# Layer 2's gather, its side bias and its scores at other places in a software-pipelined graph network kernel

## The chip, the cores and the metric

The kernel runs on one core of one Trainium2 chip. The metric is the device time of one execution in microseconds. The core has five instruction queues that run side by side and wait for each other through semaphores: TensorE (PE; its weight loads are listed apart, as PEld), VectorE (DVE), ScalarE (ACT), GpSimd (POOL) and SyncE (SP), which here only issues DMAs.

## The reference

128 graphs of 128 nodes with 384 features go through two layers of the same kind, then a residual and a layer norm.

```python
def layer(h, params):                       # h: (128, 128, 384), scanned over 2 layers
    u = einsum('bid,bjd->bij', h, h) / sqrt(D)
    a = softmax(u, axis=-1)
    delta = a * adjacency_matrix
    attn = delta / (sum(delta, axis=-1, keepdims=True) + 1e-10)
    hl, hs, hr = h @ wl.T + b_l, h @ ws.T + b_s, h @ wr.T + b_r
    ctx = (attn * upper) @ hl + diagonal(attn)[..., None] * hs + (attn * lower) @ hr
    o = (ctx - mean) / sqrt(var + 1e-12) * g + beta
    return relu(o)
out = layernorm(x + layer2(layer1(x)))      # eps 1e-5
```

All is float32. The products are formed from a high and a low part of each operand (three matmuls for one).

## The kernel before

**Tiling.** One graph is one unit of work. Per graph and layer TensorE runs 27 projection matmuls of 128 by 384: nine for each of UP, LOW and SELF (three chunks of the features, three high/low terms). UP and LOW are called the sides; they use two banks of `p_proj`, SELF a third. There are three score matmuls (128 by 256) and six gather matmuls (128 by 384), which multiply the two masked, transposed halves of the attention with the projected sides.

**Software pipeline.** Every engine has its own `iteration(i, r)`, written out by hand for the first and last iterations and rolled (four at a time) between. Iteration i works on several graphs at once: layer 1's projections of graph i, its early scores of i + 2 and i + 3, layer 2's projections of graph i - 3, its scores of i - 2, its gather of i - 4 and its output of i - 4 and i - 5. The order within a queue is the order in which the code issues; a wait holds all that is behind it in the same queue. Iterations 0 to 3 (`fill`) and from 127 on (`close`) have orders of their own. The steady order holds for iterations 4 to 126.

**TensorE's order** in one iteration: 18 side projections of layer 1 with two scores of graph i + 2 between them (`score_early`); 9 self projections of layer 1 with the three scores of layer 2 of graph i - 2 after the first, second and third (`score_late`, which first waits for `s_lo[1]`, the low part of hT of layer 2); 9 side projections of layer 2; layer 2's gather of i - 4; the other 9 side projections, with the first score of graph i + 3 after the first of them; 9 self projections of layer 2; layer 1's gather of i. A gather waits for the low attention half (`s_side_lo`, GpSimd L1300), the low projections (`s_proj_lo`, GpSimd L299), and the use of its former result.

**VectorE's order:** rows of layer 1 of graph i - 1 (L698 writes `gathered`, L702, L704, L711, L717), `low_rows` (L754), the bias of layer 1's sides (L767, which also moves them from PSUM to SBUF), the two scaled scores (L778), block transposes and masks (L817, L802, L807, L790), diagonals (L812), the bias of layer 1's self projection (L771), then `row_moments`, `row_variance` and `centre_layer2` of layer 2 (L698, L702, L704, L711, L725), the bias of layer 2's sides (L767), `output_rows` (L733, L739; it waits for the root that GpSimd computes, L1304, from what L711 wrote), and the bias of layer 2's self projection (L771).

**ScalarE's order:** `relu_rows` (L1083, three), `high_rows` (L1094), `normalise_rows` (L1066), exponentials, high halves of the attention, copies, `high_projections` of layer 1 (L1062), `keep_high` (L1033, L1034), DMA issues, the next input, squared denominators (L1099), `output_squares` (L1121, L1126), `finish` (L1066), and `high_projections` of layer 2 (L1062).

**GpSimd's order:** low projections of layer 2 (L299), root and bias for layer 1's norm (L1304, L1308), L1356, L1294 twice, low attention halves (L1300) of layer 2 and layer 1, low projections of layer 1 (L299), the root of layer 2 (L1304), the root and bias of the output (L1304, L1308), low input (L1330).

So `low_rows` hangs on this: layer 2's rows and output stand ahead of layer 1's rows in VectorE's queue, those ahead of `low_rows`, and the first layer 2 score of TensorE waits for that.

Of the kernel before, what the change touches and what calls it, by code (L numbers as in the profile page):

```python
# [52 lines left out]
def graph_block(nc: bass.Bass, xT: bass.AP, x: bass.AP, adj: bass.AP, WT: bass.AP, bias: bass.AP,  # L53
# [9 lines left out]
    with ExitStack() as ctx:  # L63
# [390 lines left out]
        def _(pe):  # L454
# [44 lines left out]
            def score_late(b1, slot1, n):  # L499

                if n == 0:
                    done(pe, s_lo[1], b1)
                    if not isinstance(b1, int) or b1 > 2:
                        done(pe, s_kept, b1 - 3)
                if n < C:
                    step = score_step(1, b1, slot1, n)
                    if n == C - 1:
                        step.then_inc(s_parts[1], 1)

            def project_sides(k, b, slot, before, b_last, steps, scored=None, first=0, last_part=14,  # L510
                              early=None):

                if 0 in steps:
                    done(pe, s_biased[before], b_last)
                for n in steps:
                    if isinstance(b, int) and b == 0 and n % 3 == 0:

                        pe.wait_ge(s_w_lo[k][UP + n // 9], n % 9 // 3 + 1)
                    last = project_step(k, b, slot, UP + n // 9, n % 9)
                    if early is not None and (n, early[2]) == (9, 0):
                        score_early(early[0], early[1], 0)
                    if early is not None and n in (1, 3, 5) and early[2] > 0 and n // 2 + early[2] <= C:
                        score_early(early[0], early[1], n // 2 + early[2] - 1)
                    if scored is not None:
                        score_slice(*scored, n, first, last_part)
                if 17 in steps:
                    last.then_inc(s_proj[k], 1)  # L530

            def project_self(k, b, slot, before, b_last, scored=None, first=0, last_part=8, late=None):
                done(pe, s_self_biased[before], b_last)
                for n in range(9):
                    if isinstance(b, int) and b == 0 and n % 3 == 0:
                        pe.wait_ge(s_w_lo[k][SELF], n // 3 + 1)
                    last = project_step(k, b, slot, SELF, n)
                    if late is not None:
                        score_late(*late, n)
                    if scored is not None and n < 8:  # L540
                        score_slice(*scored, n, first, last_part)
                last.then_inc(s_self[k], 1)
                if scored is not None:
                    score_slice(*scored, 8, first, last_part)
# [122 lines left out]
            def iteration(i, r):  # L667
                p, q = r % 2, 1 - r % 2
                if filling(i):
                    fill(i, p)  # L670
                elif closing(i):
                    close(i, p)
                else:
                    alone = isinstance(i, int) and i < 6
                    rest = (i + 2, (r + 2) % 4, 1 if alone else 2) if live(i, i + 2) else None
                    first = (i + 3, (r + 3) % 4, 0) if live(i, i + 3) and not (isinstance(i, int) and i < 5) else None
                    project_sides(0, i, r, 1, i - 4, range(18), early=rest)
                    project_self(0, i, r, 1, i - 4, late=(i - 2, p))
                    project_sides(1, i - 3, q, 0, i, range(9))
                    gather(1, i - 4)  # L680
                    project_sides(1, i - 3, q, 0, i, range(9, 18), early=first)
                    project_self(1, i - 3, q, 0, i)
                    gather(0, i, True)

            run(pe, iteration)
# [2 lines left out]
        def _(dve):  # L688
# [68 lines left out]
            def add_bias(k, b, sides_too):  # L757
# [4 lines left out]
                if sides_too:  # L762
                    if k == 0 and isinstance(b, int) and 0 < b < 4:

                        done(dve, s_proj_lo[0], b - 1)
                    done(dve, s_proj[k], b)
                    nc.vector.tensor_tensor(proj[u][:, UP:LOW + 1, :], p_proj[:, UP:LOW + 1, 0:D],  # L767
                                            bias_all[:, k, UP:LOW + 1, :], ALU.add).then_inc(s_biased[k], 1)
# [206 lines left out]
            def iteration(i, r):  # L975
# [24 lines left out]
                if live(i, i + 1):  # L1000
                    diagonal(0, i + 1, q)
                add_bias(0, i, False)
                row_moments(1, i - 4, p)
                row_variance(1, i - 4, p).then_inc(s_veps[1], 1)
                centre_layer2(i, i - 4)
                add_bias(1, i - 3, True)
                output_rows(i - 4, p)
                add_bias(1, i - 3, False)

# [3 lines left out]
        def _(act):  # L1013
# [41 lines left out]
            def high_projections(k, b):  # L1055
# [3 lines left out]
                if k == 0 and isinstance(b, int) and 0 < b < 4:  # L1059

                    done(act, s_gather[0], b - 1)
                nc.scalar.activation(proj_split[u][:, HI], proj[u][:, UP:LOW + 1, :],  # L1062
                                     ACT.Copy).then_inc(s_proj_hi[k], 1)

# [192 lines left out]
            def iteration(i, r):  # L1257
# [23 lines left out]
                if live(i, i + 1):  # L1281
                    squared_denominators(0, i + 1, q)
                squared_denominators(1, i - 3, q)
                if live(i, i - 5):
                    output_squares(i - 5, q)
                    finish(i, q)
                high_projections(1, i - 3)

            run(act, iteration)

# [187 lines left out]
```

## Time and profile before

| | |
|---|---|
| three runs | 1613.95 us median (1612.61 to 1614.08) |
| the profiled execution | 1614.73 us, span 1613.0 us |
| TensorE | 1594.6 us busy (99%), 9267 matmuls |
| VectorE | 1396.4 us (87%) |
| GpSimd | 1294.1 us (80%) |
| ScalarE | 1079.3 us (67%) |
| granted TensorE clock | 0.997 of full speed |
| DMA | 131 GB/s over the span |

The span runs from the first to the last instruction; the execution's own time has a little around it. Busy time counts each engine by itself. Matmuls are pipelined: one of 128 by 384 is recorded as about 0.34 us long and the next starts some 0.17 us after it, so their spacing is to be read from starts, and a stall can lie inside what is shown as busy. On VectorE too an operation may start before the one ahead of it has ended. In the timeline, equal instructions in a row are merged, and brackets give the idle time before a group and what released it.

### The profile page before, as it was taken

The page shows a single profiled execution, that of the slowest core. Times are in us where ns is not written, and L with a number is a line of the kernel's source. Part 1 is how long each engine was busy: PE and PEld are TensorE (multiplying, and loading weights), DVE is VectorE, ACT ScalarE, POOL GpSimd, SP SyncE. Part 2 cuts the span into 40 slices and gives each one's busy share as a digit, 9 for nine tenths or more (in the row PEclk, how much of TensorE's full clock was granted, in tenths as well). Part 3 has the DMA queues.
Part 4 walks back from the last instruction along what each step waited for, and adds up shares of the span by engine and source line. Part 5 has one row for each costly group of instructions (what it writes and reads, how often), then busy time and mean ns, then how long its engine had stood idle before and what let it go on. Part 6 is the DMA issues. An engine that isn't in the chain of part 4 may idle for free.

```text
span 1613.0 us, 35972 instructions
## 1 busy us (share of the span) xinstructions
PE 1594.6 (99%) x9267; PEld 1571.5 (97%) x9267; DVE 1396.4 (87%) x4490; ACT 1079.3 (67%) x2958; POOL 1294.1 (80%) x1665
## 2 busy tenths in 40 slices
PE   9999999999999999999999999999999999999996
PEld 8999999999999999999999999999999999999995
DVE  7788888888888888888888888888888888888887
ACT  6566666666666666666666666666666666666665
POOL 6788888888888888888888888888888888888874
PEclk9999999999999999999999999999999999999998
DMA  5555555555555555555555555555555555555541
GB/s 180 125 132 138 129 133 135 132 133 130 134 132 135 129 137 131 133 130 139 127 133 130 138 129 133 133 134 133 130 134 131 135 129 139 130 133 129 135 108 49
DMA packets 589175, 211.28 MB, mean 131 GB/s; under 512 B 473952, under 2 KB 572256, under 8 KB 589152
## 3 DMA queue, kind: packets, MB, share of 16 engines
q1 hardware_dynamic: 490752, 198.91, 47.8%
q10 hardware_dynamic: 98400, 12.11, 4.9%
q8 instruction: 9, 0.15, 0.0%
q14 instruction: 14, 0.11, 0.0%
HBM read 128.98 MB, written 81.92 MB: 131 GB/s over the span
## 4 chain that ended last, share of the span: by engine, by line
PE 97%; DVE 1%; POOL 1%; ACT 1%; issue 0%; DMA 0%; SPq 0%; DVEq 0%; POOLq 0%; ACTq 0%
PE p_proj L464 74%; PE p_gather L591 17%; PE p_score L458 5%; DMA w_raw<-WT 0%; POOL proj_split L299 0%; POOL w L1351 0%; DVE proj L767 0%; DVE p_gather L725 0%; DVE p_gather L733 0%; DVE stats L702 0%; DVE p_gather L698 0%; ACT proj_split L1062 0%; PE p_score L482 0%; DVE y L739 0%; POOL rstd L1304 0%
## 5 line engine op out<-in xcount | busy, mean ns | idle before, releaser
L464 PE MATMUL p_proj<-w,hT_layer 128*128 128x384 f32 x6912 | 1345.7, 338 | 0.0
L464 PEld LDWEIGHTS p_proj<-w,hT_layer 128*128 128x128 f32 x6912 | 1193.7, 188 | 0.5 <-POOL w L1351 0.3
L299 POOL TENSOR_TENSOR proj_split<-proj,proj_split 128x768 fp32r<-128x768 f32 x253 | 467.1, 1846 | 88.4 <-ACT proj_split L1062 88.4
L591 PE MATMUL p_gather<-proj_split,attnT_split 128*128 128x384 f32 x1536 | 322.5, 344 | 2.2 <-issue 2.2
L767 DVE TENSOR_TENSOR proj<-p_proj,bias_all 128x768 f32<-128x768 f32 x256 | 243.9, 953 | 71.6 <-PE p_proj L464 71.6
L1300 POOL TENSOR_TENSOR attnT_split<-attnT,attnT_split 128x256 fp32r<-128x256 f32 x256 | 190.2, 743 | 142.8 <-ACT attnT_split L1053 142.7
L591 PEld LDWEIGHTS p_gather<-proj_split,attnT_split 128*128 128x128 f32 x1536 | 263.0, 188 | 21.8 <-POOL attnT_split L1300 14.3
L1304 POOL TENSOR_TENSOR rstd<-veps,neg_half 128x1 f32<-128x1 f32 x384 | 208.7, 549 | 52.7 <-DVE veps L711 39.6
L1062 ACT ACTIVATE proj_split<-proj 128x768 fp32r<-128x768 f32 x256 | 213.0, 832 | 5.8 <-DVE proj L767 4.8
L458 PE MATMUL p_score<-hT_layer 128*128 128x256 f32 x768 | 215.6, 281 | 1.1 <-DVE hT_layer L754 0.8
L1066 ACT ACTIVATE normed<-gathered,nbias,rstd 128x384 f32<-128x384 f32 x128 | 90.7, 709 | 141.5 <-POOL nbias L1308 141.5
L1294 POOL TENSOR_TENSOR attnT<-whole,sides 128x256 f32<-128x256 f32 x249 | 179.1, 741 | 0.6 <-DMA whole<-swap_mem 0.6
L1066 ACT ACTIVATE o<-y,nbias,rstd 128x384 f32<-128x384 f32 x128 | 90.8, 709 | 132.5 <-POOL nbias L1308 132.5
L1133 ACT ACTIVATE hT_layer<-xt_raw 128x384 fp32r<-128x384 f32 x128 | 67.1, 525 | 141.5 <-issue 140.3
L1083 ACT ACTIVATE p_rows<-rowsT,shift,gain 128x128 f32<-128x128 f32 x369 | 149.5, 444 | 0.0
L458 PEld LDWEIGHTS p_score<-hT_layer 128*128 128x128 f32 x768 | 144.2, 188 | 1.9 <-DVE hT_layer L754 1.1
L1039 ACT ACTIVATE p_score<-scores,rows 128x128 f32<-128x128 f32 x256 | 92.7, 362 | 76.6 <-DVE rows L778 76.5
L771 DVE TENSOR_TENSOR proj<-p_proj,bias_all 128x384 f32<-128x384 f32 x256 | 141.5, 553 | 2.0 <-PE p_proj L464 1.9
L1330 POOL TENSOR_TENSOR hT_layer<-xt_raw,hT_layer 128x384 fp32r<-128x384 f32 x128 | 131.5, 1028 | 4.9 <-ACT hT_layer L1133 4.9
L802 DVE CUSTOM_DVE_ANT_0 attn<-p_score,adj_layer 128x128 f32<-128x128 f32 x256 | 70.8, 277 | 45.1 <-ACT p_score L1039 42.9
L1053 ACT ACTIVATE attnT_split<-attnT 128x256 fp32r<-128x256 f32 x256 | 103.2, 403 | 0.5 <-DVE attnT L831 0.5
L698 DVE SCALAR_TENSOR_TENSOR p_gather<-proj,rows,p_gather 128x384 f32<-128x384 f32 x128 | 79.6, 622 | 19.2 <-PE p_gather L591 12.1
(69 smaller groups left out, 1677.7 us busy)
## 6 DMA issues: line engine op xcount, KB each, us to landing
swap_mem<-blocks SPq DMA_DIRECT2D x124, 256.0 KB, 2.2
whole<-swap_mem SPq DMA_DIRECT2D x496, 64.0 KB, 2.5
xt_raw<-xT SPq DMA_DIRECT2D x128, 192.0 KB, 2.6
xn<-x SPq DMA_DIRECT2D x128, 192.0 KB, 2.6
out<-o SPq DMA_DIRECT2D x128, 192.0 KB, 2.0
rows_mem<-rows_blocks SPq DMA_DIRECT2D x123, 192.0 KB, 1.9
adj_layer<-adj SPq DMA_DIRECT2D x256, 64.0 KB, 2.1
rowsT<-rows_mem SPq DMA_DIRECT2D x246, 48.0 KB, 2.5
```

The source lines that it names most:

```text
L299: op.tensor_tensor(proj_split[u][:, LO], proj[u][:, UP:LOW + 1, :], proj_split[u][:, HI].bitcast(F32), ALU.subtract).then_inc(s_proj_lo[k], 1)
L458: return nc.tensor.matmul(parts[k], h[:, slot, HI, n, :], h[:, slot, HI:LO + 1, n, :], start=(n == 0), stop=(n == C - 1))
L464: return nc.tensor.matmul(p_proj[:, which, 0:D], hT_of(k, b)[:, slot, st, c, :], w[:, k, which, mv, c, :], start=(n == 0), stop=(n == 8))
L591: last = nc.tensor.matmul(home(k, b)[:, 0:D], AT_split[u][:, st, side, :], proj_split[u][:, mv, side, :], start=(side == UP and n == 0), s ...
L767: nc.vector.tensor_tensor(proj[u][:, UP:LOW + 1, :], p_proj[:, UP:LOW + 1, 0:D], bias_all[:, k, UP:LOW + 1, :], ALU.add).then_inc(s_biased ...
L771: nc.vector.tensor_tensor(proj[u][:, SELF, :], p_proj[:, SELF, 0:D], bias_all[:, k, SELF, :], ALU.add).then_inc(s_self_biased[k], 1)
L1062: nc.scalar.activation(proj_split[u][:, HI], proj[u][:, UP:LOW + 1, :], ACT.Copy).then_inc(s_proj_hi[k], 1)
L1066: nc.scalar.activation(rows_out, rows_in, ACT.Identity, bias=nbias[:, which:which + 1], scale=rstd[:, which:which + 1]).then_inc(s_rows, 1)
L1083: last = nc.scalar.activation(relu_T[:, c, :], rows_in[:, c, :], ACT.Relu, bias=shift1[:, c:c + 1], scale=gain1[:, c:c + 1])
L1294: nc.gpsimd.tensor_tensor(AT[k][:], whole[:, k].unsqueeze(1).broadcast_to([P, 2, N]), sides[:], ALU.mult).then_inc(s_side[k], 1)
L1300: nc.gpsimd.tensor_tensor(AT_split[u][:, LO], AT[u][:], AT_split[u][:, HI].bitcast(F32), ALU.subtract).then_inc(s_side_lo[k], 1)
L1304: return nc.gpsimd.tensor_tensor(rstd[:, which:which + 1], veps[:, which:which + 1], neg_half[:], ALU.pow)
```

## The change

Four edits. On TensorE layer 2's gather goes behind all 18 side projections of layer 2; the first score of graph i + 3 goes from the tenth side projection to behind the second self projection of layer 2; the three scores of layer 2 go from behind self projections 0, 1 and 2 of layer 1 to behind side projection 16 and self projections 0 and 2. On VectorE the bias of layer 2's sides goes ahead of `row_moments` of layer 2, with a wait for GpSimd's low projections of the graph before, which read the tile that it writes. On ScalarE `high_projections` of layer 2 goes ahead of `output_squares` and `finish`, with a wait for the gather of the graph before, which reads the tile that it writes.

```diff
                     done(pe, s_lo[1], b1)
                     if not isinstance(b1, int) or b1 > 2:
                         done(pe, s_kept, b1 - 3)
-                if n < C:
-                    step = score_step(1, b1, slot1, n)
-                    if n == C - 1:
-                        step.then_inc(s_parts[1], 1)
+                step = score_step(1, b1, slot1, n)
+                if n == C - 1:
+                    step.then_inc(s_parts[1], 1)
             def project_sides(k, b, slot, before, b_last, steps, scored=None, first=0, last_part=14,
-                              early=None):
+                              early=None, late=None):
@@ -520,23 +519,25 @@
                         pe.wait_ge(s_w_lo[k][UP + n // 9], n % 9 // 3 + 1)
                     last = project_step(k, b, slot, UP + n // 9, n % 9)
-                    if early is not None and (n, early[2]) == (9, 0):
-                        score_early(early[0], early[1], 0)
-                    if early is not None and n in (1, 3, 5) and early[2] > 0 and n // 2 + early[2] <= C:
+                    if early is not None and n in (1, 3, 5) and n // 2 + early[2] <= C:
                         score_early(early[0], early[1], n // 2 + early[2] - 1)
+                    if late is not None and n == 16:
+                        score_late(*late, 0)
                     if scored is not None:
                         score_slice(*scored, n, first, last_part)
                 if 17 in steps:
                     last.then_inc(s_proj[k], 1)
-            def project_self(k, b, slot, before, b_last, scored=None, first=0, last_part=8, late=None):
+            def project_self(k, b, slot, before, b_last, scored=None, first=0, last_part=8, early=None, late=None):
                 done(pe, s_self_biased[before], b_last)
                 for n in range(9):
                     if isinstance(b, int) and b == 0 and n % 3 == 0:
                         pe.wait_ge(s_w_lo[k][SELF], n // 3 + 1)
                     last = project_step(k, b, slot, SELF, n)
-                    if late is not None:
-                        score_late(*late, n)
+                    if early is not None and n == 1:
+                        score_early(*early, 0)
+                    if late is not None and n in (0, 2):
+                        score_late(*late, 1 + n // 2)
                     if scored is not None and n < 8:
                         score_slice(*scored, n, first, last_part)
                 last.then_inc(s_self[k], 1)
@@ -673,13 +674,12 @@
                 else:
                     alone = isinstance(i, int) and i < 6
                     rest = (i + 2, (r + 2) % 4, 1 if alone else 2) if live(i, i + 2) else None
-                    first = (i + 3, (r + 3) % 4, 0) if live(i, i + 3) and not (isinstance(i, int) and i < 5) else None
-                    project_sides(0, i, r, 1, i - 4, range(18), early=rest)
+                    first = (i + 3, (r + 3) % 4) if live(i, i + 3) and not (isinstance(i, int) and i < 5) else None
+                    project_sides(0, i, r, 1, i - 4, range(18), early=rest, late=(i - 2, p))
                     project_self(0, i, r, 1, i - 4, late=(i - 2, p))
-                    project_sides(1, i - 3, q, 0, i, range(9))
+                    project_sides(1, i - 3, q, 0, i, range(18))
                     gather(1, i - 4)
-                    project_sides(1, i - 3, q, 0, i, range(9, 18), early=first)
-                    project_self(1, i - 3, q, 0, i)
+                    project_self(1, i - 3, q, 0, i, early=first)
                     gather(0, i, True)
             run(pe, iteration)
@@ -763,6 +763,8 @@
                     if k == 0 and isinstance(b, int) and 0 < b < 4:
                         done(dve, s_proj_lo[0], b - 1)
+                    if k == 1:
+                        done(dve, s_proj_lo[1], b - 1)
                     done(dve, s_proj[k], b)
                     nc.vector.tensor_tensor(proj[u][:, UP:LOW + 1, :], p_proj[:, UP:LOW + 1, 0:D],
                                             bias_all[:, k, UP:LOW + 1, :], ALU.add).then_inc(s_biased[k], 1)
@@ -1000,10 +1002,10 @@
                 if live(i, i + 1):
                     diagonal(0, i + 1, q)
                 add_bias(0, i, False)
+                add_bias(1, i - 3, True)
                 row_moments(1, i - 4, p)
                 row_variance(1, i - 4, p).then_inc(s_veps[1], 1)
                 centre_layer2(i, i - 4)
-                add_bias(1, i - 3, True)
                 output_rows(i - 4, p)
                 add_bias(1, i - 3, False)
@@ -1059,6 +1061,8 @@
                 if k == 0 and isinstance(b, int) and 0 < b < 4:
                     done(act, s_gather[0], b - 1)
+                if k == 1:
+                    done(act, s_gather[1], b - 1)
                 nc.scalar.activation(proj_split[u][:, HI], proj[u][:, UP:LOW + 1, :],
                                      ACT.Copy).then_inc(s_proj_hi[k], 1)
@@ -1281,10 +1285,10 @@
                 if live(i, i + 1):
                     squared_denominators(0, i + 1, q)
                 squared_denominators(1, i - 3, q)
+                high_projections(1, i - 3)
                 if live(i, i - 5):
                     output_squares(i - 5, q)
                     finish(i, q)
-                high_projections(1, i - 3)
             run(act, iteration)
```

## Rows read from the trace of the kernel before

**Rows 1.** Windows, the middle 400 us: each engine's busy us (count), granted clock, DMA.
```profile
400.00:800.00 400.00, 400.00 (x2333) 395.10 (x2333) 351.21 (x1130) 271.45 (x746) 328.54 (x422) 1.00 0.54 132
```
**Rows 2.** The page's costliest groups: the gathers' weight loads; busy, mean, idle before.
```profile
L591 PEld LDWEIGHTS p_gather<-proj_split,attnT_split 128*128 128x128 f32 x1536 | 263.0, 188 | 21.8 <-POOL attnT_split L1300 14.3
```
**Rows 3.** TensorE's timeline (start, length), iterations 6 and 125.
```profile
72.99 0.28 PE L458 MATMUL p_score<-hT_layer 128*128 128x256 f32 x1
...
1543.77 0.28 PE L458 MATMUL p_score<-hT_layer 128*128 128x256 f32 x1
```
**Rows 4.** TensorE's timeline, one iteration from 1012.34.
```profile
1012.34 0.28 PE L458 MATMUL p_score<-hT_layer 128*128 128x256 f32 x1
...
1013.04 2.81 PE L464 MATMUL p_proj<-w,hT_layer 128*128 128x384 f32 x15
1015.69 1.30 PE L591 MATMUL p_gather<-proj_split,attnT_split 128*128 128x384 f32 x6
1016.83 0.34 PE L464 MATMUL p_proj<-w,hT_layer 128*128 128x384 f32 x1
...
1017.13 3.12 PE L464 MATMUL p_proj<-w,hT_layer 128*128 128x384 f32 x17
1020.08 1.20 PE L591 MATMUL p_gather<-proj_split,attnT_split 128*128 128x384 f32 x6
```
**Rows 5.** Timeline of TensorE's weight loads, the same iteration and the next score.
```profile
1015.68 0.99 PEld L591 LDWEIGHTS p_gather<-proj_split,attnT_split 128*128 128x128 f32 x6 [0.15 <-POOL attnT_split L1300]
...
1024.50 0.19 PEld L458 LDWEIGHTS p_score<-hT_layer 128*128 128x128 f32 x1
```
**Rows 6.** GpSimd's timeline, the same iteration.
```profile
1014.89 0.74 POOL L1300 TENSOR_TENSOR attnT_split<-attnT,attnT_split 128x256 fp32r<-128x256 f32 x1 [0.51 <-ACT attnT_split L1053]
...
1019.07 1.07 POOL L1304 TENSOR_TENSOR rstd<-veps,neg_half 128x1 f32<-128x1 f32 x2 [0.32 <-DVE veps L711]
1020.22 0.19 POOL L1308 TENSOR_TENSOR nbias<-neg_mean,rstd 128x1 f32<-128x1 f32 x1
...
1022.02 1.85 POOL L299 TENSOR_TENSOR proj_split<-proj,proj_split 128x768 fp32r<-128x768 f32 x1 [0.65 <-ACT proj_split L1062]
```
**Rows 7.** VectorE's timeline, the same iteration.
```profile
1012.36 0.96 DVE L767 TENSOR_TENSOR proj<-p_proj,bias_all 128x768 f32<-128x768 f32 x1 [0.55 <-PE p_proj L464]
...
1017.13 0.62 DVE L698 SCALAR_TENSOR_TENSOR p_gather<-proj,rows,p_gather 128x384 f32<-128x384 f32 x1 [0.22 <-PE p_gather L591]
...
1018.78 0.21 DVE L711 TENSOR_SCALAR veps<-eps_units,moments 128x1 f32<-128x1 f32 x1
...
1019.43 0.95 DVE L767 TENSOR_TENSOR proj<-p_proj,bias_all 128x768 f32<-128x768 f32 x1
1020.30 0.62 DVE L733 SCALAR_TENSOR_TENSOR p_gather<-p_gather,rstd,shift 128x384 f32<-128x384 f32 x1
...
1023.62 0.56 DVE L754 TENSOR_TENSOR hT_layer<-p_rows,hT_layer 128x384 fp32r<-128x384 f32 x1
```
**Rows 8.** The tail, window 1580 to 1590, columns as in rows 1.
```profile
1580.00:1590.00 10.00, 8.13 (x48) 7.32 (x47) 7.56 (x25) 5.85 (x17) 6.25 (x7) 1.00 0.21 66
```
**Rows 9.** TensorE's timeline in that window.
```profile
1588.46 0.39 PE L458 MATMUL p_score<-hT_layer 128*128 128x256 f32 x1 [0.76 <-DVE hT_layer L754]
```
**Rows 10.** ScalarE's timeline, the iteration of rows 4.
```profile
1018.44 0.60 ACT L1121 ACTIVATE spread<-y,neg_mean 128x384 f32<-128x384 f32 x1
...
1019.16 0.29 ACT L1126 ACTIVATE veps<-y_squares,out_eps 128x1 f32<-128x1 f32 x1
1020.50 0.71 ACT L1066 ACTIVATE o<-y,nbias,rstd 128x384 f32<-128x384 f32 x1 [1.05 <-POOL nbias L1308]
1021.12 0.83 ACT L1062 ACTIVATE proj_split<-proj 128x768 fp32r<-128x768 f32 x1
1021.85 1.22 ACT L1083 ACTIVATE p_rows<-rowsT,shift,gain 128x128 f32<-128x128 f32 x3
1023.10 0.49 ACT L1094 ACTIVATE hT_layer<-p_rows 128x384 fp32r<-128x384 f32 x1
```

## The prediction

> **What bounds the kernel now.** I read the windows first. In the middle 400 us TensorE is busy all the time at a granted clock of 1.00 (its level of 2.4 GHz), VectorE 351 us, GpSimd 329 us, ScalarE 271 us [rows 1]. So the order of TensorE's stream is the kernel, and any time in which it runs without a gap can only be shortened by a gap that "busy" hides. The costliest groups show one: the weight loads of the gathers were idle 21.8 us, 14.3 of it for GpSimd's attnT_split [rows 2]. TensorE's timeline gives the loop: the first layer 2 score of iteration 6 starts at 72.99, that of iteration 125 at 1543.77, so 1470.78 / 119 = 12.36 us each [rows 3]. Inside one iteration [rows 4] projections follow each other at 2.65 / 15 = 0.177 or 2.95 / 17 = 0.174 us, a score 0.12 (1017.13 - 1016.83, less one projection). Layer 2's gather (x6 at 1015.69) is 1.30 us long, layer 1's (x6 at 1020.08) 1.20, by the same six matmuls. The 0.10 is the late weight load: it starts at 1015.68 after 0.15 idle, released by the GpSimd operation that ends at 1014.89 + 0.74 = 1015.63 [rows 5, 6]. That is the only repeated stall of TensorE: 0.10 x 123 = 12 us, 0.8% of the time.
>
> VectorE is next, and its order matters more than its share. One loop of it [rows 7] idles 0.55 ahead of the bias of layer 1's sides (L767, for TensorE), and then runs nearly without a gap to low_rows (L754), which ends at 1023.62 + 0.56 = 1024.18. The weight load of the first layer 2 score, which needs it, starts at 1024.50 [rows 5]. So the slack of that hand-over is 0.32 us.
>
> **The change, part by part.**
> *Gather of layer 2 behind all 18 side projections.* Its GpSimd input has been ready since 1015.63, and the gather would begin nine projections later: the stall goes, -0.10 an iteration. The number of matmuls is unchanged (54 + 12 + 6). For VectorE the gather's result comes later, and that is not hidden by itself; it is in the sum below.
>
> *VectorE: bias of layer 2's sides ahead of layer 2's rows.* In order on VectorE now: bias of layer 1's own projection (L771), bias of layer 2's sides, and then row_moments (L698), variance, centre, output rows, L771, row_moments of layer 1, low_rows. The bias waits for TensorE's 18th side projection and L698 for the gather behind that. All that stands behind L698 in VectorE's queue waits with it: the output, the bias that frees p_proj, layer 1's rows, and low_rows. The added wait on s_proj_lo[1] is for a GpSimd operation of the iteration before, ended some 4 us earlier in the loop (1022.02 + 1.85 there); I cost it at nothing, with one wait step of 0.10 as its other end.
>
> *First layer 2 score two projections earlier* (behind n = 16 of the sides, the others behind n = 0 and 2 of the self projection). The last of the three stays where it was, so the ScalarE copies behind it don't move; but the first now wants low_rows 2 x 0.175 = 0.35 us sooner. The slack of 0.32 is gone by this edit alone. The bias of layer 1's sides comes one score, 0.12, later.
>
> *Chunk 0 of layer 1's early score* moves from the tenth side projection to n = 1 of the self projection. It waits for keep_high, whose ScalarE copies are at the start of the loop's middle; it comes later, and gets only more cover. Nothing.
>
> *ScalarE: high_projections of layer 2 ahead of output_squares and finish, with a wait for the gather of layer 2.* The queue behind it is output_squares, finish, relu_rows, high_rows; priced under the rivals. SP's queue isn't reordered: its out transfer waits for finish and goes out later, and xn behind it is wanted an iteration later.
>
> **The sum: one loop from the first layer 2 score to the next.** All times are counted from that score's start, with durations of the kernel before.
> 1. To the start of the gather's last matmul: 3 scores x 0.12, and 28 projections (the last of the sides, 9 self, 18 of layer 2's sides) and 5 gather matmuls x 0.175: 0.36 + 5.78 = 6.14 [rows 4].
> 2. From there to L698: before, the last gather matmul started at 1016.83 - 0.18 = 1016.65 and L698 at 1017.13: 0.48. Sum 6.62 [rows 4, 7]. VectorE is free by then: the sides' bias starts at 6.14 - 6 x 0.175 + 0.37 = 5.46 and takes 0.87 (1019.43 to 1020.30), so 6.33.
> 3. From L698 to the output rows (L733): without a wait 1019.43 - 1017.13 = 2.30. But L733 needs GpSimd's root. Before, the bias of the sides stood between and hid it. Now: L698 to variance (L711) 1018.78 - 1017.13 = 1.65, to the root's start 0.29, the root 0.55 (two take 1.07), and the release 0.14 (as from the gather's end, 1015.69 + 1.30 = 1016.99, to L698): 2.63. Sum 9.25 [rows 6, 7].
> 4. L733 to the end of low_rows: 1023.62 - 1020.30 + 0.56 = 3.88. Sum 13.13 [rows 7].
> 5. Release of the weight load 0.05 (1015.63 to 1015.68), and 0.11 from a held load to its matmul: a score that waited for this same L754 near the end took 0.39 where others take 0.28. Sum 13.29 [rows 5, 9].
>
> TensorE alone would be back at that score after 12.26 us, so it would stand still there for 1.03 us in each iteration, and the sum is 13.29 - 12.36 = +0.93 an iteration. The check from the other side, counted from an iteration's first projection: the gather and with it L698 come 9 x 0.175 - 0.10 = 1.47 later, the bias that no longer stands between gives back 0.87, the root costs 0.33, so low_rows is 0.93 late; the score is 0.35 early, the loop without its stall 0.10 shorter, and 0.32 of slack is used up: a stall of 1.06, and +0.96 an iteration with the stall that is gone. The two agree to 0.03.
>
> Iterations 4 to 126 have this order, so there are 122 loops: 122 x 0.93 = 113. The profiled execution took 1614.7 (span 1613.0), 0.8 above the median of the runs; 1614.7 + 113 - 0.8 = 1727 us.
>
> Ends: if the root is not waited for (2.30 in step 3) and all matmuls keep to 0.173, the loop is 12.90, +0.54 x 122 = +66: 1680. If two of the new waits cost a step of 0.10 more each, 13.50: +139, 1753. I take the middle reckoning because each of its steps has a row of its own kind.
>
> **A rule weighed.** In the tail of this trace TensorE was busy 8.13 us of a stretch of 10, with a wait of 0.76 before one score, and the granted clock stayed 1.00 [rows 8, 9]. The Trainium skill, "TensorE: Matmul & The Clock Gate", section "A second HAM failure mode: psum-queue depth-cycling", says that small idle gaps between groups of matmuls, if frequent, can make the clock swing between its two levels. By the row the 1.03 us gap costs itself alone; by the rule more, and that is the last rival.
>
> **The rivals.**
> *ScalarE's chain sets low_rows instead.* Behind the gather (6.14 + 0.34 + 0.07 = 6.55): high_projections 0.73, squares 0.72 + 0.29, ready at 8.29; GpSimd's two roots start at 6.62 + 1.65 + 0.29 = 8.56, nbias 1.15 later and 0.19 long, 9.90; finish starts at 9.99, relu_rows 0.62 later, high_rows 1.25 after that and 0.49 long: 12.35 [rows 6, 10]. Low_rows could start at 12.38, where VectorE itself comes at 12.57. If the root's wait in step 3 is smaller than reckoned, VectorE comes at 12.24 and this chain sets the loop: 13.10, +0.74 x 122 = +90, 1704. For: it is only 0.19 behind. Same sign.
> *Faster.* Place: the first layer 2 score. If low_rows is in time for it, TensorE never stops and the gain is the old stall, 0.10 x 122 = 12 us: 1602. The point from which it decides: the slack is 0.32 - 0.35 - 0.10 = -0.13, so low_rows would have to end 0.13 us earlier in the iteration than now, and every 0.01 us later than that costs 1.2 us in all. For it speaks the idle 0.55 ahead of L767, which says that VectorE has time to give; against, that this idle lies behind low_rows, and the waits added are ahead of it.
> *Next to no change.* With VectorE's new order free of cost, the score held by its own shift alone (0.13), the loop would be 12.26 + 0.13 = 12.39: +0.03 x 122 = 4, 1618.
> *The clock swings.* Were a tenth of an iteration's 66 wide matmuls at the lower level, twice as long: 6.6 x 0.175 = 1.2 us more, 122 x 1.2 = +141 on 1727: about 1870.
>
> **How the numbers follow.** VectorE's loop 0.70, ScalarE's chain 0.19 (both slower, 1680 to 1753), faster 0.06, no change 0.03, clock 0.02. Range: 1675 to 1753, which leaves out some 15 in 100. Within 0.2% (3 us, about what a measurement of this kernel can tell from none) 0.03; faster 0.06; slower 0.91.
>
> **What would show it.** Right: the gather's six matmuls are 1.20 long; the score L458 waits about 1.0 us for VectorE's L754 in each iteration, and TensorE's busy share falls to 92 or 93%; L698 waits for the gather, L733 for the root; finish starts 10.0 behind that score (8.2 now, 1020.50 - 1012.34); the clock 1.00. Wrong: no wait at L458, or the first wait of TensorE at another place (self projections for L771, the gather for GpSimd), or low_rows released by ScalarE (the second case).

## The result, and the profile after

The changed kernel takes 1705.72 us (median of 5 runs, 1705.23 to 1707.88) against 1613.95: a ratio of 1.0574, 95% interval 1.0558 to 1.0589. It is 92 us slower; 1727 was forecast, range 1675 to 1753. The profiled execution took 1707.0 us, span 1705.3, at a mean clock of 0.998.

The window of the middle 400 us, columns as in [rows 1], shows TensorE busy 95%, with the clock still 1.00:

```profile
400.00:800.00 400.00, 381.53 (x2197) 371.67 (x2196) 334.94 (x1073) 257.61 (x705) 308.93 (x398) 1.00 0.51 125
```

The list of who waited for whom (us in total, times, longest; waits under 0.15 us are not in it) names the place. First TensorE's weight loads, then its matmuls:

```profile
PEld p_score L458 <- DVE hT_layer L754: 85.4, 93, 2.1
PEld p_score L458 <- issue: 28.4, 31, 1.2
```

```profile
PE p_score L458 <- DVE hT_layer L754: 74.1, 122, 1.8
```

These are 122 waits for low_rows, one in each iteration from 5 on, 0.61 us each by the matmuls' records (74.1 / 122) and 0.9 by the loads' (113.8 / 124). The gather's wait for GpSimd is gone from the list. The forecast had given TensorE a busy share of 92 or 93%, from a stall of 1.03. It shows 95%, since part of each stall lies inside the matmul records, which are longer than the spacing; the loads' 0.9 and the loop below are the better measure. TensorE's timeline around one loop:

```profile
74.42 0.39 PE L458 MATMUL p_score<-hT_layer 128*128 128x256 f32 x1 [1.76 <-DVE hT_layer L754]
...
1004.74 0.39 PE L458 MATMUL p_score<-hT_layer 128*128 128x256 f32 x1 [0.65 <-DVE hT_layer L754]
...
1005.91 4.41 PE L464 MATMUL p_proj<-w,hT_layer 128*128 128x384 f32 x24
1010.15 1.21 PE L592 MATMUL p_gather<-proj_split,attnT_split 128*128 128x384 f32 x6
...
1017.84 0.39 PE L458 MATMUL p_score<-hT_layer 128*128 128x256 f32 x1 [0.55 <-DVE hT_layer L754]
...
1634.04 0.39 PE L458 MATMUL p_score<-hT_layer 128*128 128x256 f32 x1 [0.55 <-DVE hT_layer L754]
```

The scores at 74.42 and 1634.04 are those of iterations 6 and 125 and give the loop, (1634.04 - 74.42) / 119 = 13.11 us, where [rows 3] had 12.36; 0.75 more, times 122 loops, is 91 us, the whole difference. Layer 2's gather is 1.21 long, where [rows 4] had 1.30 and 1.20 for layer 1's. VectorE's timeline in that loop (L769 is now the bias of the sides, L773 that of the self projection), against [rows 7]:

```profile
1005.34 0.96 DVE L769 TENSOR_TENSOR proj<-p_proj,bias_all 128x768 f32<-128x768 f32 x1 [0.65 <-PE p_proj L464]
...
1009.47 0.55 DVE L773 TENSOR_TENSOR proj<-p_proj,bias_all 128x384 f32<-128x384 f32 x1
1010.42 0.96 DVE L769 TENSOR_TENSOR proj<-p_proj,bias_all 128x768 f32<-128x768 f32 x1 [0.40 <-PE p_proj L464]
1011.49 0.62 DVE L698 SCALAR_TENSOR_TENSOR p_gather<-proj,rows,p_gather 128x384 f32<-128x384 f32 x1
...
1013.03 0.21 DVE L711 TENSOR_SCALAR veps<-eps_units,moments 128x1 f32<-128x1 f32 x1
1013.16 0.62 DVE L725 SCALAR_TENSOR_TENSOR p_gather<-p_gather,moments,gain 128x384 f32<-128x384 f32 x1
1013.91 0.63 DVE L733 SCALAR_TENSOR_TENSOR p_gather<-p_gather,rstd,shift 128x384 f32<-128x384 f32 x1
...
1017.24 0.55 DVE L754 TENSOR_TENSOR hT_layer<-p_rows,hT_layer 128x384 fp32r<-128x384 f32 x1
```

Read it from the bottom: low_rows ends at 1017.24 + 0.55 = 1017.79, the score behind it starts at 1017.84. From L698 on VectorE stops only for the root. L733 starts 0.75 behind L725, where in e8_self_bias_ahead below the next operation starts 0.53 behind it, so this wait is 0.22. L698 itself starts 0.13 behind the gather's end (1010.15 + 1.21 = 1011.36), as it did before (0.14). Behind the bias it could have started at 1010.42 + 0.87 = 1011.29 (0.87 as in [rows 7]), so it is the late gather that it waits for, by 0.20; 0.29 was forecast. GpSimd and ScalarE (L1308 root, L1312 nbias; L1070 finish, L1098 high_rows):

```profile
1013.33 1.06 POOL L1308 TENSOR_TENSOR rstd<-veps,neg_half 128x1 f32<-128x1 f32 x2 [1.60 <-DVE veps L711]
```

```profile
1014.75 0.71 ACT L1070 ACTIVATE o<-y,nbias,rstd 128x384 f32<-128x384 f32 x1 [1.53 <-POOL nbias L1312]
1015.37 1.21 ACT L1087 ACTIVATE p_rows<-rowsT,shift,gain 128x128 f32<-128x128 f32 x3
1016.61 0.49 ACT L1098 ACTIVATE hT_layer<-p_rows 128x384 fp32r<-128x384 f32 x1
```

The row holds two roots; the first, 0.55 long, ends at 1013.88 and L733 starts at 1013.91; high_rows ends at 1017.10, only 0.14 ahead of low_rows.

### The profile page after: what moved, and what is told of

The parts are those of the page before. It is cut to its first block, busy times and chain, and to the rows that moved or that the text cites. A ratio compares the mean times of both kernels' runs of the same rounds, so it can differ in the third digit from the quotient of the medians.

```text
span 1705.3 us, 36226 instructions
## 1 busy us (share of the span) xinstructions
PE 1611.8 (95%) x9267; PEld 1567.5 (92%) x9267; DVE 1414.3 (83%) x4490; ACT 1086.4 (64%) x2958; POOL 1289.5 (76%) x1665
## 4 chain that ended last, share of the span: by engine, by line
POOL 29%; issue 24%; DVE 22%; ACT 16%; PE 6%; DVEq 1%; ACTq 1%; DMA 1%; POOLq 0%; SPq 0%
POOL proj_split L299 16%; POOL rstd L1308 6%; ACT proj_split L1066 5%; POOL attnT_split L1304 5%; ACT attnT_split L1055 4%; ACT p_score L1041 4%; DVE p_gather L733 4%; PE p_proj L464 3%; DVE stats L702 3%; DVE gathered L698 3%; DVE hT_layer L754 3%; DVE proj L773 3%; PE p_score L458 2%; ACT crossed L1027 2%; DVE scores L780 2%
## 5 line engine op out<-in xcount | busy, mean ns | idle before, releaser
L464 PEld LDWEIGHTS p_proj<-w,hT_layer 128*128 128x128 f32 x6912 | 1177.3, 188 | 2.3 <-POOL w L1355 1.0
L299 POOL TENSOR_TENSOR proj_split<-proj,proj_split 128x768 fp32r<-128x768 f32 x253 | 467.7, 1849 | 7.5 <-ACT proj_split L1066 7.5
L1308 POOL TENSOR_TENSOR rstd<-veps,neg_half 128x1 f32<-128x1 f32 x384 | 206.6, 548 | 214.8 <-DVE veps L711 199.1
L769 DVE TENSOR_TENSOR proj<-p_proj,bias_all 128x768 f32<-128x768 f32 x256 | 245.3, 958 | 137.0 <-PE p_proj L464 135.3
L592 PE MATMUL p_gather<-proj_split,attnT_split 128*128 128x384 f32 x1536 | 308.9, 335 | 2.5 <-issue 2.5
L458 PE MATMUL p_score<-hT_layer 128*128 128x256 f32 x768 | 228.9, 298 | 74.7 <-DVE hT_layer L754 74.1
L592 PEld LDWEIGHTS p_gather<-proj_split,attnT_split 128*128 128x128 f32 x1536 | 270.4, 188 | 3.3 <-issue 3.3
L1066 ACT ACTIVATE proj_split<-proj 128x768 fp32r<-128x768 f32 x256 | 214.4, 838 | 6.2 <-DVE proj L769 4.6
L1070 ACT ACTIVATE o<-y,nbias,rstd 128x384 f32<-128x384 f32 x128 | 90.8, 710 | 188.0 <-POOL nbias L1312 188.0
L1070 ACT ACTIVATE normed<-gathered,nbias,rstd 128x384 f32<-128x384 f32 x128 | 90.8, 710 | 152.3 <-POOL nbias L1312 152.3
L773 DVE TENSOR_TENSOR proj<-p_proj,bias_all 128x384 f32<-128x384 f32 x256 | 141.5, 553 | 2.0 <-PE p_proj L464 1.9
L733 DVE SCALAR_TENSOR_TENSOR p_gather<-p_gather,rstd,shift 128x384 f32<-128x384 f32 x128 | 80.1, 626 | 16.4 <-POOL rstd L1308 0.6
```

The costliest lines, as they stand in the source:

```text
L299: op.tensor_tensor(proj_split[u][:, LO], proj[u][:, UP:LOW + 1, :], proj_split[u][:, HI].bitcast(F32), ALU.subtract).then_inc(s_proj_lo[k], 1)
L458: return nc.tensor.matmul(parts[k], h[:, slot, HI, n, :], h[:, slot, HI:LO + 1, n, :], start=(n == 0), stop=(n == C - 1))
L464: return nc.tensor.matmul(p_proj[:, which, 0:D], hT_of(k, b)[:, slot, st, c, :], w[:, k, which, mv, c, :], start=(n == 0), stop=(n == 8))
L592: last = nc.tensor.matmul(home(k, b)[:, 0:D], AT_split[u][:, st, side, :], proj_split[u][:, mv, side, :], start=(side == UP and n == 0), s ...
L773: nc.vector.tensor_tensor(proj[u][:, SELF, :], p_proj[:, SELF, 0:D], bias_all[:, k, SELF, :], ALU.add).then_inc(s_self_biased[k], 1)
L1070: nc.scalar.activation(rows_out, rows_in, ACT.Identity, bias=nbias[:, which:which + 1], scale=rstd[:, which:which + 1]).then_inc(s_rows, 1)
```

## The experiments

The theory is the forecast's: one loop from the first layer 2 score over gather, layer 2's rows, output, layer 1's rows and low_rows back to that score sets the time. Its rivals are that a single edit costs the 92 us, or VectorE's load as such.

**e1_scores_back.** The changed kernel with the scores at their old places:

```diff
-                    if late is not None and n == 16:
-                        score_late(*late, 0)
...
-                    if late is not None and n in (0, 2):
-                        score_late(*late, 1 + n // 2)
+                    if late is not None and n < C:
+                        score_late(*late, n)
```

> The changed kernel with layer 2's three scores back behind self projections 0, 1 and 2 of layer 1; gather, VectorE's and ScalarE's order as changed. My theory (a loop from the first layer 2 score over gather, layer 2's rows, output, layer 1's rows and low_rows back to that score sets the time): the loop has two projections less, 13.10 - 0.35 = 12.75 us, so 0.39 x 122 = 48 over the kernel before, 1662 us (1655 to 1670). Rival (the early score alone is what costs, VectorE's new order is free): TensorE's own 12.26, 1602 us. Rival (the score's place doesn't matter since VectorE is the bound as such): 1706 us.

Measured 1658.48 us, ratio 1.0282 (1.0264 to 1.0299); loop 12.76. The two projections are worth 0.35 a loop, as the theory has it; both rivals fall. The scores' places are about half of the loss (46 of 92 us, each against the kernel before as it was timed beside the run: 1612.93 and 1613.95), and a loss without them remains.

**e2_scores_only.** The kernel before with the same three places:

```diff
+                    if late is not None and n == 16:
+                        score_late(*late, 0)
...
-                    if late is not None:
-                        score_late(*late, n)
+                    if late is not None and n in (0, 2):
+                        score_late(*late, 1 + n // 2)
```

> The kernel before with only the three scores moved. My theory: the loop over low_rows is 12.36 at most, but the bias of layer 1's sides and with it the late attention halves come one score (0.12) later, so the gather's stall grows from 0.10 to 0.22 and the loop to 12.47: +13, 1627 us (1618 to 1632), with waits at the gather for GpSimd. Rival (the early score alone costs what the change costs): 1706 us. Rival (it costs its 0.03 of missing slack only, and the gather's wait isn't on that chain): 1614 to 1618 us.

Measured 1633.87 us, ratio 1.0131 (1.0114 to 1.0148); loop 12.49. This is just above the range, by the mechanism named: not low_rows but the gather's input is waited for, now 0.30 a loop (36.7 / 122) in place of the 0.15 of [rows 5] (waits of the weight loads):

```profile
PEld p_gather L593 <- POOL attnT_split L1302: 36.7, 122, 0.3
```

The same edit costs 21 us here and 46 in the changed kernel: it depends on which loop it lies on.

**e3_bias_back.** The changed kernel with VectorE's old order:

```diff
-                add_bias(1, i - 3, True)
                 row_moments(1, i - 4, p)
                 row_variance(1, i - 4, p).then_inc(s_veps[1], 1)
                 centre_layer2(i, i - 4)
+                add_bias(1, i - 3, True)
                 output_rows(i - 4, p)
```

> The changed kernel with VectorE's bias of layer 2's sides back behind centre_layer2; gather late and scores early as changed. My theory: the bias stands again between layer 2's rows and low_rows (0.87), but hides the wait for GpSimd's root (0.23 with the smaller aggregate gap): the loop is 13.74 us, +0.64 x 122 = 78 on the changed kernel, 1784 us (1765 to 1795). Rival (the bias ahead is what costs): faster than the changed kernel, 1614 to 1690 us.

Measured 2187.71 us, ratio 1.3567 (1.3545 to 1.3590); loop 17.07. The sign is right, the size is far off (1784 was expected); the reckoning had left out ScalarE. With high_projections ahead of the squares, all of ScalarE's queue waits for the late bias (L769), and low_rows for that queue (ScalarE's, then VectorE's, then TensorE's timeline):

```profile
1025.34 0.85 ACT L1066 ACTIVATE proj_split<-proj 128x768 fp32r<-128x768 f32 x1 [4.19 <-DVE proj L769]
```

```profile
1028.47 0.14 DVE L717 TENSOR_SCALAR neg_mean<-moments 128x1 f32<-128x1 f32 x1
1030.56 0.56 DVE L754 TENSOR_TENSOR hT_layer<-p_rows,hT_layer 128x384 fp32r<-128x384 f32 x1 [1.94 <-ACT hT_layer L1098]
```

```profile
1008.30 0.62 PE L464 MATMUL p_proj<-w,hT_layer 128*128 128x384 f32 x2 [0.60 <-DVE proj L769]
...
1014.12 0.58 PE L458 MATMUL p_score<-hT_layer 128*128 128x256 f32 x1 [2.35 <-DVE hT_layer L754]
...
1020.82 1.20 PE L592 MATMUL p_gather<-proj_split,attnT_split 128*128 128x384 f32 x6
```

And the clock: behind that idle time of 2.35 the granted clock is 0.50, the lower level of 1.2 GHz, and this once in each loop; over the middle 400 us it is 0.90 (windows):

```profile
400.00:800.00 400.00, 332.26 (x1693) 317.60 (x1694) 254.45 (x824) 199.31 (x543) 236.75 (x306) 0.90 0.39 96
1014.00:1016.50 2.50, 2.38 (x8) 2.38 (x9) 1.50 (x8) 0.89 (x2) 2.42 (x5) 0.50 0.35 116
```

From the score to the gather's last matmul it takes 1020.82 + 0.87 - 1014.12 = 7.57, against 1010.15 + 0.87 - 1004.74 = 6.28 in the changed kernel, by the same instructions in the same order: 1.29 more. Without ScalarE low_rows would have begun 0.06 behind L717, as it does in the changed kernel (by the start of L717 there, 1017.18); it began 1030.56 - 1028.47 = 2.09 behind it, so ScalarE held it 2.03. The expected loop and these two make 13.74 + 2.03 + 1.29 = 17.06, against the 17.07.

**f2_gather_alone.** So VectorE's order was priced without ScalarE's: e1_scores_back with `add_bias(1, i - 3, True)` on VectorE and `high_projections(1, i - 3)` on ScalarE back at their old places, which leaves of the change the late gather, the first score of graph i + 3 behind it, and the two added waits. A first try, e6_gather_only, had kept that score at the tenth side projection:

```diff
-                    project_sides(1, i - 3, q, 0, i, range(9))
-                    gather(1, i - 4)
-                    project_sides(1, i - 3, q, 0, i, range(9, 18), early=first)
+                    project_sides(1, i - 3, q, 0, i, range(18), early=first)
+                    gather(1, i - 4)
```

> The kernel before with layer 2's gather behind all 18 side projections, nothing else: VectorE's and ScalarE's orders and the scores' places are those of before. My theory: from the first score 3 scores, 26 projections and 5 gather matmuls to the gather's last (5.79), 0.48 to layer 2's rows, 3.06 to the output with the bias of the sides between, 3.88 to the end of low_rows, 0.16 to the score: 13.37 us, +1.01 x 122 = 123, 1736 us (1720 to 1750). Against the changed kernel with the scores back (1658) that prices VectorE's new order at a gain of about 78 us. Rival (VectorE's new order is what costs, the late gather alone only removes the stall): 1602 to 1615 us.

That took 1874.95 us, ratio 1.1609 (1.1592 to 1.1627), since the score now stood ahead of the gather and waited for ScalarE's copy (0.73 in the row below), which the gather used to cover. It doesn't measure what it was meant to. It shows what the edit that I priced at nothing is for: against f2_gather_alone below, leaving that score where it was costs 1874.95 - 1742.44 = 133 us, 1.09 a loop.

```profile
1008.37 0.35 PE L458 MATMUL p_score<-hT_layer 128*128 128x256 f32 x1 [0.73 <-ACT p_gather L1033]
```

> The gather behind all 18 side projections with the early score of graph i + 3 behind the second self projection as in the changed kernel; VectorE's and ScalarE's orders and layer 2's scores as before. My theory, as for e6_gather_only, whose score stood ahead of the gather: a loop of 13.37 us, 1736 us (1720 to 1750). Against e1_scores_back (1658) that is VectorE's and ScalarE's new order as a gain of 78 us. Rival (their new order costs): 1602 to 1650 us.

Measured 1742.44 us, ratio 1.0785 (1.0769 to 1.0802); loop 13.42, forecast 13.37. TensorE's stall now shows at two places. The first projections of the next iteration wait for the bias of layer 2's sides, which frees `p_proj` and is late too; the score behind them still waits for low_rows (L752 here), so that hand-over still sets the loop (waits of the weight loads, then ScalarE's and VectorE's timelines):

```profile
PEld p_proj L464 <- DVE proj L767: 112.0, 122, 1.0
PEld p_score L458 <- DVE hT_layer L752: 31.8, 94, 1.1
```

```profile
1011.57 0.49 ACT L1096 ACTIVATE hT_layer<-p_rows 128x384 fp32r<-128x384 f32 x1
1012.10 0.56 DVE L752 TENSOR_TENSOR hT_layer<-p_rows,hT_layer 128x384 fp32r<-128x384 f32 x1
```

In this loop low_rows starts 0.04 behind high_rows' end (1012.06), so ScalarE's queue releases it, 0.1 behind what VectorE alone would do; the two queues are that close. Each against the kernel before as timed beside the run (1615.29, 1612.93, 1613.95): the late gather alone costs 127 us, VectorE's and ScalarE's new order gives back 82 (127 to 46), and the scores' places take 46 (46 to 92).

**e7_scalar_back** and **e8_self_bias_ahead** test the second chain, ScalarE's, which was reckoned to be just behind. Both start from the changed kernel:

```diff
-                high_projections(1, i - 3)
                 if live(i, i - 5):
                     output_squares(i - 5, q)
                     finish(i, q)
+                high_projections(1, i - 3)
```

> The changed kernel with ScalarE's high_projections of layer 2 back behind finish. My theory: finish still waits for GpSimd's nbias, and the 0.73 us of high_projections now stand between finish and relu_rows, so high_rows ends at 17.84 where low_rows began at 17.24 (the loop from 1004.74): ScalarE's chain sets low_rows, the loop is 13.73 us, +0.63 x 122 = 77 on the changed kernel, 1783 us (1765 to 1790). The clock stays at its upper level. Rival (ScalarE is off the path): 1706 us.

Measured 1782.79 us, ratio 1.1040 (1.1023 to 1.1057); loop 13.75, and low_rows is released by high_rows (waits of VectorE):

```profile
DVE hT_layer L754 <- ACT hT_layer L1098: 66.4, 122, 0.6
```

The second:

```diff
                 centre_layer2(i, i - 4)
+                add_bias(1, i - 3, False)
                 output_rows(i - 4, p)
-                add_bias(1, i - 3, False)
```

> The changed kernel with VectorE's bias of layer 2's self projection ahead of output_rows, so that it covers the wait for GpSimd's root (0.22). My theory: VectorE alone would reach low_rows 0.24 earlier, but ScalarE's high_rows ends only 0.11 ahead of it, so the loop loses 0.11: 12.99 us, 1692 us (1688 to 1697), low_rows released by ScalarE. Rival (ScalarE's chain is further behind than I read): 0.24, 1676 us. Rival (the root's wait costs nothing): 1706 us.

Measured 1693.81 us, ratio 1.0490 (1.0474 to 1.0506); loop 13.01, 0.10 less than the changed kernel's. In its timelines high_rows ends at 1008.38 + 0.49 = 1008.87 and low_rows starts at 1008.90, where VectorE alone could have begun 0.14 earlier (0.06 behind L717):

```profile
1008.38 0.49 ACT L1098 ACTIVATE hT_layer<-p_rows 128x384 fp32r<-128x384 f32 x1
```

```profile
1008.70 0.14 DVE L717 TENSOR_SCALAR neg_mean<-moments 128x1 f32<-128x1 f32 x1
1008.90 0.56 DVE L754 TENSOR_TENSOR hT_layer<-p_rows,hT_layer 128x384 fp32r<-128x384 f32 x1
```

**e4_low_rows_first.** Can the changed order be freed of its loop?

```diff
-                normalise_layer1(i - 1, q)
                 low_rows(i - 2, p)
+                normalise_layer1(i - 1, q)
...
-                relu_rows(i, i - 2, p)
-                high_rows(i - 2, p)
+                if isinstance(i, int) and i == 4:
+                    relu_rows(i, i - 2, p)
+                    high_rows(i - 2, p)
...
                     output_squares(i - 5, q)
+                relu_rows(i + 1, i - 1, q)
+                high_rows(i - 1, q)
+                if live(i, i - 5):
                     finish(i, q)
```

> The changed kernel with low_rows ahead of layer 1's rows on VectorE, and on ScalarE relu_rows and high_rows of that graph between output_squares and finish of the iteration before, so that low_rows needs not wait for them. My theory: the loop over low_rows is cut; it is ready about 1 us before the score needs it, TensorE never stops, and the gather's stall stays gone: 12.26 us a loop, 1602 us (1598 to 1612), busy share 99%. Rival (VectorE's in-order waits of some 1 us a loop are the bound by themselves): its ordered work of 11.35 us and its idle times give 12.5 to 13.1 us, 1630 to 1706 us.

Measured 1646.28 us, ratio 1.0208 (1.0191 to 1.0226); loop 12.61. The score's wait is gone, so that loop was the bound; but the forecast of 1602 is missed, and the time lies in the rival's range. By the timelines layer 1's rows, now behind low_rows, start 0.46 later (1004.79 to 1005.25); they feed GpSimd's root, which stands ahead of cross_sum in its queue. VectorE waits 0.8 a loop (96.4 / 121) for cross_sum, and TensorE 0.36 (42.2 / 118) for VectorE's self bias, about what the loop is above the expected 12.26 (waits of VectorE and of the weight loads). That the late rows cause these waits is read from the order of the queues and not tested by a run of its own:

```profile
DVE neg_mean L747 <- POOL cross_sum L1362: 96.4, 121, 0.9
```

```profile
PEld p_proj L464 <- DVE proj L773: 42.2, 118, 0.5
```

**f1_gather_one_later.** The stall of the kernel before was worth one projection, not nine:

```diff
-                    project_sides(1, i - 3, q, 0, i, range(9))
+                    project_sides(1, i - 3, q, 0, i, range(10))
                     gather(1, i - 4)
-                    project_sides(1, i - 3, q, 0, i, range(9, 18), early=first)
+                    project_sides(1, i - 3, q, 0, i, range(10, 18), early=first)
```

with the first score of graph i + 3 at n = 10. The first try, e5_gather_one_later, left that score at n = 9, ahead of the gather, and took 1707.96 us, ratio 1.0577 (1.0563 to 1.0592), by the wait of e6_gather_only, here 0.61 a loop.

> The kernel before with layer 2's gather behind the tenth side projection of layer 2 in place of the ninth, nothing else. My theory: the weight load was 0.15 late, one projection is 0.17, so the stall of 0.10 goes; layer 2's rows come 0.07 later, inside the slack of low_rows (0.32): 12.26 us a loop, 1602 us (1600 to 1606). Rival (the stall follows the gather, since its input hangs on TensorE's own order): 1613 us.

> The kernel before with layer 2's gather behind the tenth side projection of layer 2 and the early score of graph i + 3 behind the first projection after the gather, as before (the run e5_gather_one_later had left that score ahead of the gather, where it waits for ScalarE's copy L1034). My theory: the stall of 0.10 goes and nothing else changes: 12.26 us a loop, 1602 us (1600 to 1607). Rival (the stall follows the gather): 1613 us.

Measured 1601.78 us, ratio 0.9919 (0.9906 to 0.9933); loop 12.24. No steady wait is left on TensorE: in its list none has more than six occurrences.

**f3_gather_and_apart.** f1_gather_one_later, and:

```diff
-                    if late is not None:
-                        score_late(*late, n)
+                    if late is not None and n % 2 == 0:
+                        score_late(*late, n // 2)
```

> The kernel before with layer 2's gather behind the tenth side projection (early score of graph i + 3 behind the next) and layer 2's three scores behind self projections 0, 2 and 4 of layer 1: two projections apart without being earlier. My theory: besides the stall of 0.10, the projections behind the scores go at 173.4 to 174.1 ns in place of 176.5 (as in e2_scores_only), 15 x 0.0025 to 0.003 = 0.04 to 0.05 a loop, perhaps as much again in the 17 that follow layer 2's gather: 12.21 us, 1596 us (1592 to 1602). Rival (the spacing has to do with other things): as f1_gather_one_later, 1602 us.

Measured 1597.00 us, ratio 0.9890 (0.9875 to 0.9905); loop 12.21. It is the fastest version here, 1.1% ahead of the kernel before. The projections between the last of the three scores and layer 2's gather (TensorE's timelines; f1_gather_one_later first) go at (1006.00 - 1003.17) / 16 = 0.177 there and (1004.00 - 1001.56) / 14 = 0.174 here. The loop is 0.03 shorter, 4 of the 5 us between the two runs:

```profile
1003.17 2.99 PE L464 MATMUL p_proj<-w,hT_layer 128*128 128x384 f32 x16
1006.00 1.21 PE L591 MATMUL p_gather<-proj_split,attnT_split 128*128 128x384 f32 x6
```

```profile
1001.56 2.60 PE L464 MATMUL p_proj<-w,hT_layer 128*128 128x384 f32 x14
1004.00 1.23 PE L591 MATMUL p_gather<-proj_split,attnT_split 128*128 128x384 f32 x6
```

## Why the prediction was right

The mechanism is the one that was forecast: a loop over low_rows, held by the late gather and the root.

- *The stall of 0.10 goes.* Right: the gather is 1.21 long, and f1_gather_one_later gains 13.5 us by that alone.
- *Steps 1 and 2, to L698.* Forecast 6.62, and 0.11 of step 5 that the records have at the loop's start: 6.73. Measured 1011.49 - 1004.74 = 6.75.
- *Step 3, L698 to L733.* The one term that was mis-sized: 2.63 forecast, 1013.91 - 1011.49 = 2.42 measured. L711 came 1.54 behind L698 in place of 1.65, and the root's release took 0.03 in place of the 0.14 taken from the gather's. That is 0.21 x 122 = 26 us, more than the whole miss of 21. The first half was there to be read: the 1.65 is from one iteration, and of the 128 in the trace of before 98 have 1.54, the iteration ahead of that one among them:

```profile
1004.80 0.62 DVE L698 SCALAR_TENSOR_TENSOR p_gather<-proj,rows,p_gather 128x384 f32<-128x384 f32 x1
1006.34 0.21 DVE L711 TENSOR_SCALAR veps<-eps_units,moments 128x1 f32<-128x1 f32 x1
```

- *Step 4.* 3.88 forecast, 1017.79 - 1013.91 = 3.88 measured. *Step 5.* 0.05 and 0.11 (0.39 against 0.28), both as forecast. *The added waits*, put at nothing, cost nothing: the lists have one of 1.6 us (L769 for GpSimd's L299) and one of 1.0 (L1066 for a gather) in the whole run.
- *The earlier score costs its 0.35 in full*, since the slack was spent: e1_scores_back. *The chunk of the early score* is free where the change puts it, and only there.
- *The rival that ScalarE's chain sets low_rows.* Its 13.10 a loop and 1704 us are what was measured, to 2 us, and yet it is not what happened; by the time alone the two can't be told apart. High_rows ends 0.14 ahead of low_rows, and in e8_self_bias_ahead the loop shortens by 0.10 when only VectorE's queue is relieved, which it couldn't if ScalarE's set it. e7_scalar_back and e8_self_bias_ahead, each right to 2 us, show that ScalarE's chain is next. Its place was reckoned well partly by luck: finish came 10.01 behind the score (9.99 reckoned) and high_rows' end 12.36 (12.35), because the 0.11 of the held score at the start, left out there, and the 0.11 by which L711 came sooner cancel.
- *The other rivals.* *Faster* failed at the point named: low_rows ended later, not earlier. *The clock* stayed at 1.00 with a gap of 0.6 to 0.9 us a loop. So what the section "A second HAM failure mode: psum-queue depth-cycling" of the Trainium skill's "TensorE: Matmul & The Clock Gate" describes, a clock that swings with frequent small gaps, did not come about with gaps of this size.

Not separated is how VectorE's and ScalarE's orders share the 82 us that they give back.

## What to carry to other kernels

A hand-over between two in-order engines is a loop; add up its durations along both queues before moving anything, since the busy share (VectorE fell from 88 to 84% here) says nothing of it. A stall of 0.15 us wants one instruction of 0.17 behind which to hide, not nine: what goes further arrives later for everyone downstream. And what stands behind a moved instruction in its own queue moves too, even where it has another purpose (the early score in e5_gather_one_later).

## What the runs showed of the hardware

In e3_bias_back, after TensorE's idle time of 2.35 us, with another of 0.60 in the same loop, the granted clock was at its lower level (0.50) in the stretch that followed. In e7_scalar_back, with waits of 1.23 us a loop (149.8 / 122), it stayed at 1.00. Which of the two gaps in e3_bias_back brought the clock down, or whether it took both, no run here tells. The rows of e7_scalar_back are these (waits of TensorE, then a window):

```profile
PE p_score L458 <- DVE hT_layer L754: 149.8, 122, 1.5
```

```profile
400.00:800.00 400.00, 364.31 (x2099) 355.09 (x2098) 322.63 (x1020) 243.99 (x669) 294.50 (x379) 1.00 0.48 119
```

The spacing of the 128 by 384 matmuls differed with what ran before them: with only one projection between two scores, the projections that followed averaged 0.177 us in f1_gather_one_later, with two between them 0.174 in f3_gather_and_apart. Why, no run here tells.
